# Cross-attention and a routed feed-forward block on one core: another order for the input transposes, the block product and its scaling

## The chip, the core and the metric

The kernel runs on one core of one Trainium2 chip. The metric is device time in microseconds (us), the median of several runs. Before the change it is 903.54 us (three runs, 903.44 to 903.98). Five queues of instructions run side by side, each in its own order: TensorE (PE in the profile, with its weight loads PEld), VectorE (DVE), ScalarE (ACT), GpSimd (POOL) and SyncE (SP), which here only issues DMAs. They meet at semaphores.

## What is computed

The input x has 128 batch elements of 128 rows by 256 features; ctx has the same shape. Per batch element:

```python
x = x + xattn(layernorm(x), ctx)   # 16 heads of 16: q from x, k and v from ctx
                                   # softmax over axis=2 of bhqk: over the QUERIES
x = x + ffn(layernorm(x))          # scores = x @ w_router; the 96 best rows of 128 become
                                   # gelu(row @ w_block), the other 32 rows stay as they are
```

## The kernel before, in words

**Slots.** Batch elements go through a software pipeline. One slot of the loop, `s`, runs the scores of element `s`, the attention of `s - 1`, the output projection and residual of `s - 2`, the transposes of the residual stream of `s - 3`, the block product (feed-forward weight) of `s - 4`, GELU of `s - 5` to `s - 7`, the routing of a group of eight elements, the final sum of `s - 16`, and, ahead of time, the normalising and transposing of the inputs of `s + 8`. Slots 0 and 1 and part of 2 and 3 are the start-up, written out by hand. Nothing plans the order at run time: each engine's function lists its calls by hand, the loops over `s` on PE (L567), ACT (L727), DVE (L1033), POOL (L1278) and SP (L310) each give one slot, and all else is semaphore waits. In the flag `sure` (slots 20 to 119 on PE) some waits are dropped that others imply.

**What the change and the prediction's steps touch.**

- `transpose_inputs` (L397, PE): four 128x128 transposes of the normalised input and of ctx into `ps_t`. `inputs_high` (L653, ACT) casts `ps_t` to the high part `t_hi`, `inputs_low` (L868, DVE) makes the rest, `t_lo`.
- `block_product` (L472, PE): six matmuls of 258 columns, also into `ps_t`. `product_scaled` (L931, DVE) scales it by the row's `rstd2` into `z_sb`. One PSUM bank thus serves the inputs and the product in turn.
- `queries_or_keys` (L504, PE): in each slot one half of the queries or keys of the next four elements, six matmuls of 512 columns into `ps_q`. `queries` or `keys` (L901, L913, DVE) empties the bank. `transpose_x1` (L417, PE) writes into the same bank and waits for that.
- `values` (L456), `projection` (L518), `scores` (L372), `attention` (L437): the other PE steps.
- `maxima` (L800, DVE): four reductions a slot, one for each quarter of the scores; `exps` (L635, ACT): four calls of four exponentials, the last quarter of element `s - 1` in slot `s`.
- `residual` (L821, DVE), then `stats2_of_pair` (L830, DVE): statistics for the second normalisation, once for two elements, in odd slots at the end. `stats1_of_pair` (L847): the same for inputs, in even slots.
- `rstd1_of_pair` (L1131), `rstd2_of_pair` (L1174, both POOL): powers from these statistics. `values_over_sums` (L1160, POOL) divides the values by the softmax sums into `v_pad`, which the attention matmuls need. `scaled_values_ready` (L433, PE) is the wait for it.
- `router` (L950, DVE): eleven steps spread over eight slots.

The order of PE in a slot before, and of POOL:

```python
scores(s); transpose_inputs(s + LEAD); values(s - 1); queries_or_keys(s); keep_columns; candidates
projection(s - 2); block_product(s - 4); scaled_values_ready(s - 1); transpose_x1(s - 3); attention(s - 1)

normalise(s + 9); rstd1_of_pair(s + 11); rstd2_of_pair(s - 4); gelu_square; values_over_sums(s - 1)
unprocessed; gelu_factor; gelu_sum; input_and_bias; gelu_cubic(s - 5); gelu_product(s - 7)
```

Of the kernel before, what the change touches and what calls it, by code (L numbers as in the profile page):

```python
# [6 lines left out]
def cross_attention_routed_ffn(  # L7
# [20 lines left out]
    B, T, E = x.shape  # L28
# [22 lines left out]
    with ctx:  # L51
# [93 lines left out]
        def has(b):  # L145
            return 0 <= b < B
# [86 lines left out]
        def _(sp):  # L233
# [64 lines left out]
            load_x(10)  # L298
            load_x(12)
            load_x(14)  # L300
            load_c(8)
            load_c(10)
            queries_even_odd_of_pair(2)
            load_c(12)
            load_c(14)
            queries_even_odd_of_pair(4)
            load_x(16)
            queries_even_odd_of_pair(6)
# [14 lines left out]
        def _(pe):  # L323
# [73 lines left out]
            def transpose_inputs(b, settled=False):  # L397
# [3 lines left out]
                if not settled:  # L401
                    inputs_ready(b)
                if has(b - LEAD - 5):
                    pe.wait_ge(z_ready, upto(b - LEAD - 5))
                elif 2 <= b <= 4:
                    pe.wait_ge(t_lo_ready, upto(b - 2))
                elif b > 4:
                    pe.wait_ge(t_lo_ready, upto(b - 1))
# [63 lines left out]
            def block_product(b, settled=False):  # L472
# [3 lines left out]
                if not settled:  # L476
                    pe.wait_ge(xt_ready, upto(b))
                pe.wait_ge(t_lo_ready, upto(b + LEAD + 4))
                if has(b - 1) and not has(b + LEAD + 4):
                    pe.wait_ge(z_ready, upto(b - 1))  # L480
# [86 lines left out]
            for s in range(2, B - 1):  # L567
                sure = 20 <= s < B - 8
                scores(s)
                if s < 4:  # L570
                    transpose_inputs(2 * s + 4)
                else:
                    transpose_inputs(s + LEAD, s > 4)
                values(s - 1)
                if s < 4:
                    queries_or_keys_of_pair(2 * s, 1)
                else:
                    queries_or_keys(s)
                keep_columns(s - 16)
                candidates(s - 12)  # L580
                projection(s - 2, sure)
                queries_and_keys_ready(s + 1)
                if s < 4:
                    transpose_inputs(2 * s + 5)
                if s == 2:
                    queries_or_keys_of_pair(6, 0)
                if s >= 4:
                    inputs_ready(s + LEAD + 1)
                block_product(s - 4, sure)
                if sure:  # L590
                    scaled_values_ready(s - 1)
                transpose_x1(s - 3, sure)
                router_bank_free(s + 1)
                attention(s - 1, sure)

            scores(B - 1)
            values(B - 2)
            projection(B - 3)
            block_product(B - 5)
            transpose_x1(B - 4)  # L600
# [17 lines left out]
        def _(act):  # L618
# [108 lines left out]
            for s in range(2, B):  # L727
                sure = 20 <= s < B - 1
                x1_high(s - 4, sure)
                exps(s - 1, 0, halves=(0,))  # L730
                attention_copy(s - 2, sure)
                exps(s - 1, 0, halves=(1,))
                gelu_tanh(s - 7)
                inputs_high(s + LEAD if s >= 4 else 2 * s + 4)
                exps(s, 3, sure)
                exps(s, 2)
                if s < 4:
                    inputs_high(2 * s + 5)
                exps(s, 1)
# [31 lines left out]
        def _(dve):  # L771
# [158 lines left out]

            def product_scaled(b, settled=False):  # L931

                if has(b):
                    dve.wait_ge(z_mm, upto(b))
                    if not settled:
                        dve.wait_ge(rstd2_ready, upto(b))
                    if b % 2 == 0 and has(b - R):
# [95 lines left out]
            for s in range(2, B):  # L1033
                sure = 20 <= s < B - 1
                x1_low(s - 4)
                if s == 3:
                    block_weights_low()
                router(s - 13, 2)
                router(s - 14, 4)
# [5 lines left out]
                values_and_bias(s - 1, sure)  # L1045
                inputs_low(s + LEAD if s >= 4 else 2 * s + 4)
                inverse_sums_01(s - 1)
# [10 lines left out]
                maxima(s, 0)  # L1058
                if s < 4:
                    inputs_low(2 * s + 5)  # L1060
                if s == 2:
# [10 lines left out]
                if s >= 4:  # L1072
                    stats1_of_pair(s + 12)
                product_scaled(s - 4, sure)
                if s < 4:
# [43 lines left out]
        def _(pool):  # L1119
# [8 lines left out]
            nc.gpsimd.memset(q_eo[:, 0, :, :, 2:4, :], 0.0).then_inc(q_eo_zero, 1)  # L1128
            nc.gpsimd.memset(q_eo[:, 1, :, :, :, :], 0.0).then_inc(q_eo_zero, 1)

# [128 lines left out]
            input_and_bias(0)  # L1259
            input_and_bias(1)  # L1260
            rstd1_of_pair(6)
            normalise(6)
# [7 lines left out]
            for s in range(2, 4):  # L1270
# [4 lines left out]
                input_and_bias(s + 2)  # L1275
            rstd1_of_pair(14)

            for s in range(4, B):  # L1278
                sure = 20 <= s < B - 1
                normalise(s + LEAD + 1, sure)  # L1280
                rstd1_of_pair(s + 11)
                rstd2_of_pair(s - 4)
                gelu_square(s - 5, sure)
# [4 lines left out]
                gelu_sum(s - 7)  # L1288
                input_and_bias(s + 2)
                gelu_cubic(s - 5)  # L1290
                gelu_product(s - 7)

            rstd2_of_pair(B - 4)
            gelu_factor(B - 5)
# [43 lines left out]
```

## Time and profile before

| | |
|---|---|
| median of three runs | 903.54 us |
| the profiled execution | 904.1 us, of which its span (first to last instruction) 902.3 us |
| busy share of the span | PE 96%, DVE 95%, ACT 96%, POOL 88% |
| granted TensorE clock, mean | 0.991 of full speed |
| DMA engines | 26.4% for the kernel's main queue |

How to read the rows below. A timeline row has the start in us, the length in us, the engine, the line, the operation, what is written and read, shapes, how many like instructions are merged (x16), and in brackets the idle time of the engine just before it and who ended it. Matmuls overlap in the pipeline, so the time that one costs is the distance from its start to the start of the next. On ACT, DVE and POOL a row's length also contains some overlap with the next row. A window row has the stretch, its length, then busy us (and instructions) of PE, PEld, DVE, ACT and POOL, the granted clock, and share and GB/s of the DMA engines. A wait row has the us in total, the times, and the longest.

### The profile page before, as it was taken

Reading aid. Unit: us, or ns where it says so; the run is one execution under the profiler, and the core shown is the slowest. Engines: PE = TensorE matmul, PEld = TensorE weight load, DVE = VectorE, ACT = ScalarE, POOL = GpSimd, SP = SyncE. Lnnn points to the kernel's source line nnn. Section 1 sums busy time; section 2 is a strip of 40 time slices with the busy share of each in tenths; the row PEclk is TensorE's granted clock in tenths of the full one; section 3 lists DMA queues with packets and bytes.
Section 4 is the critical chain, followed back from the end, with each engine's and each line's share of the span. In section 5 each row is a group of like instructions: output and inputs, shape, how many; then the busy total and the mean of one; then the engine's idle time right before and its main releaser. Section 6 shows DMA issues by size and latency. Waiting matters only on the chain. (4 is left out here: it accounts for less than half of the span.)

```text
span 902.3 us, 30174 instructions
## 1 busy us (share of the span) xinstructions
PE 864.8 (96%) x9842; PEld 718.8 (80%) x9842; DVE 857.9 (95%) x2068; ACT 870.6 (96%) x4632; POOL 789.6 (88%) x1489
## 2 busy tenths in 40 slices
PE   6999999999999999999999999999999999999972
PEld 6778888888888888888888888888888888888752
DVE  5888999999999999999999999999999999999987
ACT  4999999999999999999999999999999999999984
POOL 5468879999999999999999999999999999998865
PEclk9999999999999999999999999999999999999997
DMA  7221123232323232223333222323222323211102
GB/s 233 69 65 53 54 63 86 79 93 59 84 82 89 72 96 69 79 79 85 84 83 91 57 80 88 91 72 95 61 85 79 87 78 90 75 40 40 41 24 94
DMA packets 71357, 70.40 MB, mean 78 GB/s; under 512 B 12064, under 2 KB 63520, under 8 KB 71200
## 3 DMA queue, kind: packets, MB, share of 16 engines
q1 hardware_dynamic: 69840, 67.68, 26.4%
q8 instruction: 79, 1.29, 0.6%
q10 hardware_dynamic: 1360, 0.79, 0.3%
q14 instruction: 78, 0.64, 0.2%
HBM read 35.13 MB, written 16.78 MB: 58 GB/s over the span
## 5 line engine op out<-in xcount | busy, mean ns | idle before, releaser
L646 ACT ACTIVATE e_sb<-ps_s,neg_max 128x128 f32<-128x128 f32 x2048 | 772.1, 639 | 2.8 <-DVE neg_max L805 2.7
L646 ACT ACTIVATION_READ_ACCUMULATOR e_sb<-ps_s,neg_max 128x1 f32 x2048 | 718.2, 464 | 0.0
L805 DVE TENSOR_REDUCE neg_max<-ps_s 128x4 f32<-128x512 f32 x512 | 331.0, 666 | 19.7 <-PE ps_s L385 18.2
L385 PE MATMUL ps_s<-q_eo,k_sb 32*128 32x256 f32 x2048 | 146.6, 399 | 3.6 <-ACT e_sb L646 1.5
L450 PE MATMUL ps_a<-e_sb,v_pad 128*32 128x128 f32 x4096 | 138.4, 276 | 1.5 <-POOL v_pad L1168 0.9
L344 PE MATMUL ps_a<-w_o_sb,o_sb 128*128 128x256 f32 x512 | 131.7, 379 | 4.0 <-DVE v_sb L929 3.8
L450 PEld LDWEIGHTS ps_a<-e_sb,v_pad 128*32 128x32 f32 x4096 | 104.1, 109 | 23.2 <-issue 21.5
L385 PEld LDWEIGHTS ps_s<-q_eo,k_sb 32*128 32x128 f32 x2048 | 95.8, 184 | 32.9 <-issue 28.7
L344 PEld LDWEIGHTS ps_a<-w_o_sb,o_sb 128*128 128x128 f32 x512 | 93.8, 189 | 22.8 <-issue 4.7
L1157 POOL TENSOR_TENSOR x_sb<-x_sb,bo_sb 128x256 f32<-128x256 f32 x128 | 105.1, 822 | 0.2
L1168 POOL TENSOR_TENSOR v_pad<-v_sb,recip 128x256 f32<-128x256 f32 x128 | 79.5, 621 | 29.1 <-DVE recip L865 27.1
L657 ACT CAST t_hi<-ps_t 128x512 fp32r<-128x512 f32 x126 | 94.3, 748 | 7.5 <-PE ps_t L414 7.0
L688 ACT ACTIVATE g_sb<-g_sb 128x256 f32<-128x256 f32 x128 | 99.0, 774 | 1.4 <-POOL g_sb L1215 1.4
L337 PE MATMUL ps_t<-w_z_hi,xt_hi 128*128 128x258 f32 x256 | 96.4, 377 | 2.2 <-DVE z_sb L941 2.2
L665 ACT COPY o_sb<-ps_a 128x256 f32<-128x256 f32 x128 | 91.1, 712 | 2.4 <-PE ps_a L450 2.4
L633 ACT CAST xt_hi<-ps_q 128x256 fp32r<-128x256 f32 x128 | 88.4, 691 | 1.4 <-PE ps_q L430 1.4
L1215 POOL TENSOR_TENSOR g_sb<-g_sb,z_sb 128x256 f32<-128x256 f32 x128 | 88.3, 690 | 0.3
L873 DVE TENSOR_TENSOR t_lo<-ps_t,t_hi 128x512 fp32r<-128x512 f32 x126 | 85.2, 676 | 2.7 <-ACT t_hi L657 2.6
L337 PE MATMUL ps_a<-w_v_hi,t_hi 128*128 128x256 f32 x256 | 83.2, 325 | 0.7 <-DVE w_z_sb L797 0.7
L1229 POOL TENSOR_TENSOR z_sb<-g_sb,z_sb 128x256 f32<-128x256 f32 x121 | 82.8, 684 | 0.0
L1198 POOL TENSOR_TENSOR g_sb<-z_sb 128x256 f32<-128x256 f32 x123 | 75.3, 612 | 0.0
L337 PE MATMUL ps_a<-w_v_lo,t_hi 128*128 128x256 f32 x256 | 72.5, 283 | 0.0
(113 smaller groups left out, 2213.8 us busy)
## 6 DMA issues: line engine op xcount, KB each, us to landing
x_sb<-in_x SPq DMA_DIRECT2D x64, 256.0 KB, 3.0
c_sb<-in_ctx SPq DMA_DIRECT2D x64, 256.0 KB, 3.0
out<-z_sb SPq DMA_DIRECT2D x64, 256.0 KB, 2.4
q_eo<-q_raw SPq DMA_DIRECT2D x504, 32.0 KB, 2.0
z_sb<-in_L_xattn_Wkv ACTq DMA_DIRECT2D x2, 256.0 KB, 6.7
z_sb<-in_L_xattn_Wq ACTq DMA_DIRECT2D x1, 256.0 KB, 3.6
w_z_sb<-in_L_ffn_w_block SPq DMA_DIRECT2D x1, 256.0 KB, 8.0
w_o_sb<-in_L_xattn_Wo SPq DMA_DIRECT2D x1, 256.0 KB, 7.1
```

Source lines behind the costliest of these rows:

```text
L337: last = nc.tensor.matmul(dst, lhs(a, c), rhs(b, c), start=(c == 0 and n == 0), stop=(c == C - 1 and n == len(terms) - 1))
L344: last = nc.tensor.matmul(dst, lhs(c), rhs(c), start=(c == 0), stop=(c == C - 1))
L385: mm = nc.tensor.matmul(ps_s[:, bank(b, j), c, :, :], k_sb[rows, r2, c, h * T:(h + 1) * T], q_eo[rows, r2, :, c, h, :], start=True, stop=True)
L450: mm = nc.tensor.matmul(ps_attn[32 * j:32 * j + 32, c * T:(c + 1) * T], v_pad[:, b % 2, c * J + j, par:par + 2, :].rearrange("p a d -> p ( ...
L633: nc.scalar.copy(xt_hi[:, b % 2, :], ps_xt).then_inc(xt_hi_ready, 1)
L646: last = nc.scalar.activation(e_sb[:, b % 3, j, c, par, :], ps_s[:, bank(b, j), c, par, :], ACT.Exp, bias=neg_max[:, b % 4, h:h + 1], accu ...
L657: nc.scalar.copy(t_hi[:, n, :, :, h * T:(h + 1) * T].rearrange("p k c t -> p (k c) t"), inputs_bank(b)[:, :].rearrange("p (n t) -> p n t", ...
L665: nc.scalar.copy(o_sb[:, b % 2, :], ps_attn).then_inc(o_ready, 1)
L688: nc.scalar.activation(g_sb[:, b % 4, :], g_sb[:, b % 4, :], ACT.Tanh, scale=SLOPE).then_inc(tanh_ready, 1)
L805: nc.vector.tensor_reduce(neg_max[:, b % 4, :].rearrange("p (c j q) -> p j c q", c=C, j=J)[:, j, :, :], ps_s[:, bank(b, j), :, :, :], AX.X ...
L1157: nc.gpsimd.tensor_tensor(x_sb[:, b % RX, :], x_sb[:, b % RX, :], bo_sb[:, :], ALU.add).then_inc(xb_ready, 1)
L1215: nc.gpsimd.tensor_tensor(g_sb[:, b % 4, :], g_sb[:, b % 4, :], z_sb[:, b % R, 0:E], ALU.mult).then_inc(cubic_ready, 1)
```

## The change

On PE, the transposes of the inputs go from behind the scores to the end of the slot, between the transposes of the residual stream and the attention. The block product goes from behind the projection to a place between the values and the queries or keys. On DVE its scaling goes from the end of the slot to a place between the second and the third maximum, and the low part of the inputs goes to the top of the slot. On ACT the cast of the inputs goes to the top of the slot, and the last quarter of the exponentials is no longer split by the copy of the attention. On POOL `rstd2_of_pair` goes from before `values_over_sums` of the next slot to a place ahead of `gelu_cubic`, and `rstd1_of_pair` from odd to even slots. The bounds of two waits move by one. In the start-up SP issues some loads behind the queries' DMAs instead of ahead of them, one memset of POOL comes later, and the second inputs of slots 2 and 3 are cast a slot later.

```diff
 sync (start-up)
             load_x(12)
+            queries_even_odd_of_pair(2)
+            load_c(8)
             load_x(14)
-            load_c(8)
             load_c(10)
-            queries_even_odd_of_pair(2)
+            queries_even_odd_of_pair(4)
             load_c(12)
+            load_x(16)
             load_c(14)
-            queries_even_odd_of_pair(4)
-            load_x(16)
             queries_even_odd_of_pair(6)
 tensor: transpose_inputs(b)
-                if has(b - LEAD - 5):
-                    pe.wait_ge(z_ready, upto(b - LEAD - 5))
+                if has(b - LEAD - 4):
+                    pe.wait_ge(z_ready, upto(b - LEAD - 4))
 tensor: block_product(b)
-                pe.wait_ge(t_lo_ready, upto(b + LEAD + 4))
+                pe.wait_ge(t_lo_ready, upto(b + LEAD + 3))
 tensor: loop over s
                 scores(s)
                 if s < 4:
                     transpose_inputs(2 * s + 4)
-                else:
-                    transpose_inputs(s + LEAD, s > 4)
                 values(s - 1)
+                block_product(s - 4, sure)
...
                 projection(s - 2, sure)
                 queries_and_keys_ready(s + 1)
-                if s < 4:
-                    transpose_inputs(2 * s + 5)
-                if s == 2:
-                    queries_or_keys_of_pair(6, 0)
                 if s >= 4:
-                    inputs_ready(s + LEAD + 1)
-                block_product(s - 4, sure)
+                    inputs_ready(s + LEAD)
                 if sure:
                     scaled_values_ready(s - 1)
                 transpose_x1(s - 3, sure)
+                transpose_inputs(s + LEAD if s >= 4 else 2 * s + 5, s >= 4)
                 router_bank_free(s + 1)
                 attention(s - 1, sure)
+                if s == 2:
+                    queries_or_keys_of_pair(6, 0)
             scores(B - 1)
             values(B - 2)
+            block_product(B - 5)
             projection(B - 3)
-            block_product(B - 5)
 scalar: loop over s
                 x1_high(s - 4, sure)
-                exps(s - 1, 0, halves=(0,))
+                if s == 3:
+                    inputs_high(9)
+                elif s >= 4:
+                    inputs_high(s + LEAD - 1)
                 attention_copy(s - 2, sure)
-                exps(s - 1, 0, halves=(1,))
+                exps(s - 1, 0)
                 gelu_tanh(s - 7)
-                inputs_high(s + LEAD if s >= 4 else 2 * s + 4)
+                if s < 4:
+                    inputs_high(2 * s + 4)
                 exps(s, 3, sure)
                 exps(s, 2)
-                if s < 4:
-                    inputs_high(2 * s + 5)
                 exps(s, 1)
 vector: loop over s
                 x1_low(s - 4)
                 if s == 3:
                     block_weights_low()
+                    inputs_low(9)
+                elif s >= 4:
+                    inputs_low(s + LEAD - 1)
...
                 maxima(s, 3)
                 maxima(s, 2)
                 router(s - 16, 9)
                 values_and_bias(s - 1, sure)
-                inputs_low(s + LEAD if s >= 4 else 2 * s + 4)
+                if s < 4:
+                    inputs_low(2 * s + 4)
+                product_scaled(s - 4)
                 inverse_sums_01(s - 1)
                 maxima(s, 1)
...
                 maxima(s, 0)
-                if s < 4:
-                    inputs_low(2 * s + 5)
...
                 stats2_of_pair(s - 3)
                 if s >= 4:
                     stats1_of_pair(s + 12)
-                product_scaled(s - 4, sure)
 gpsimd (start-up)
-            nc.gpsimd.memset(q_eo[:, 1, :, :, :, :], 0.0).then_inc(q_eo_zero, 1)
...
             input_and_bias(1)
+            nc.gpsimd.memset(q_eo[:, 1, :, :, :, :], 0.0).then_inc(q_eo_zero, 1)
             rstd1_of_pair(6)
...
-            rstd1_of_pair(14)
+            rstd2_of_pair(0)
 gpsimd: loop over s
                 normalise(s + LEAD + 1, sure)
-                rstd1_of_pair(s + 11)
-                rstd2_of_pair(s - 4)
+                rstd1_of_pair(s + 10)
                 gelu_square(s - 5, sure)
                 values_over_sums(s - 1, sure)
...
                 input_and_bias(s + 2)
+                rstd2_of_pair(s - 3)
                 gelu_cubic(s - 5)
                 gelu_product(s - 7)
 gpsimd (end)
-            rstd2_of_pair(B - 4)
```

`product_scaled` also waits for `rstd2_ready` in every slot now, where it left that wait out in the `sure` ones.

## Rows read from the trace of the kernel before

**Rows 1.** Busy time by engine in a stretch of eight slots.

```profile
448.74:502.22 53.48, 53.20 (x621) 44.27 (x615) 52.67 (x130) 53.48 (x293) 49.97 (x96) 1.00 0.29 81
```

**Rows 2.** Timeline of PE in slot 66, up to the scores of slot 67.

```profile
462.89 1.15 PE L385 MATMUL ps_s<-q_eo,k_sb 32*128 32x256 f32 x16
...
465.19 0.39 PE L337 MATMUL ps_q<-t_hi,w_k_hi 128*128 128x512 f32 x1
...
466.34 0.39 PE L337 MATMUL ps_q<-t_lo,w_k_hi 128*128 128x512 f32 x1
466.56 1.02 PE L344 MATMUL ps_a<-w_o_sb,o_sb 128*128 128x256 f32 x4
...
467.55 0.28 PE L337 MATMUL ps_t<-w_z_hi,xt_lo 128*128 128x258 f32 x1
...
468.15 0.38 PE L430 MATMUL ps_q<-ident,x_sb 128*128 128x128 f32 x2
468.46 1.08 PE L450 MATMUL ps_a<-e_sb,v_pad 128*32 128x128 f32 x32
469.47 1.15 PE L385 MATMUL ps_s<-q_eo,k_sb 32*128 32x256 f32 x16
```

**Rows 3.** Timeline of DVE in slot 67, an odd slot.

```profile
470.76 1.29 DVE L805 TENSOR_REDUCE neg_max<-ps_s 128x4 f32<-128x512 f32 x2 [0.23 <-PE ps_s L385]
...
473.57 0.74 DVE L918 TENSOR_SCALAR k_sb<-ps_q,bk_sb 128x512 f32<-128x512 f32 x1
474.23 0.41 DVE L827 TENSOR_TENSOR x_sb<-ps_a,x_sb 128x256 f32<-128x256 f32 x1
...
475.62 0.70 DVE L834 BATCH_NORM_STATS2 st<-x_sb 128x6 f32<-128x512 f32 x1
```

**Rows 4.** Timeline of POOL in slots 67 and 68.

```profile
470.12 0.64 POOL L1215 TENSOR_TENSOR g_sb<-g_sb,z_sb 128x256 f32<-128x256 f32 x1
...
471.97 0.19 POOL L1136 TENSOR_SCALAR ve<-st 128x2 f32<-128x2 f32 x1
...
473.68 0.62 POOL L1168 TENSOR_TENSOR v_pad<-v_sb,recip 128x256 f32<-128x256 f32 x1
...
476.62 0.72 POOL L1215 TENSOR_TENSOR g_sb<-g_sb,z_sb 128x256 f32<-128x256 f32 x1
...
478.65 0.19 POOL L1179 TENSOR_SCALAR ve<-st 128x2 f32<-128x2 f32 x1
...
479.65 0.61 POOL L1198 TENSOR_TENSOR g_sb<-z_sb 128x256 f32<-128x256 f32 x1
```

**Rows 5.** Timelines where one engine was released by another: DVE, PE; DVE, POOL.

```profile
403.42 0.46 DVE L941 TENSOR_SCALAR z_sb<-ps_t,rstd 128x258 f32<-128x258 f32 x1
...
403.94 0.44 PE L414 MATMUL ps_t<-ident,xhat 128*128 128x128 f32 x2 [0.19 <-DVE z_sb L941]
...
874.78 0.69 DVE L834 BATCH_NORM_STATS2 st<-x_sb 128x6 f32<-128x512 f32 x1
...
875.63 0.19 POOL L1179 TENSOR_SCALAR ve<-st 128x2 f32<-128x2 f32 x1 [1.07 <-DVE st L834]
```

**Rows 6.** Groups of instructions by line: a router step (mean ns of one).

```profile
L967 DVE MAX8 top<-cand 8x8 f32<-8x128 f32 x64 | 17.5, 273 | 0.4
```

**Rows 7.** Start-up: timelines of ACT, PE and POOL, and a wait of SP.

```profile
38.05 0.59 ACT L657 CAST t_hi<-ps_t 128x512 fp32r<-128x512 f32 x1 [0.69 <-PE ps_t L414]
...
46.17 0.59 ACT L657 CAST t_hi<-ps_t 128x512 fp32r<-128x512 f32 x1 [0.87 <-PE ps_t L414]
...
48.31 1.15 PE L385 MATMUL ps_s<-q_eo,k_sb 32*128 32x256 f32 x16 [0.94 <-ACT e_sb L646]
...
25.01 0.19 POOL L1136 TENSOR_SCALAR ve<-st 128x2 f32<-128x2 f32 x1 [9.04 <-DVE st L851]
...
SPq L263 <- DVE q_raw L886: 4.5, 1, 4.5
```

**Rows 8.** Busy time by engine in two early stretches; the granted clock follows the five engines.

```profile
11.00:15.20 4.20, 3.88 (x20) 3.88 (x21) 2.43 (x5) 1.11 (x3) 3.60 (x8) 0.59 1.11 356
...
20.50:27.30 6.80, 4.32 (x37) 3.44 (x36) 5.88 (x13) 6.06 (x36) 2.10 (x5) 1.00 0.16 35
```

More of the change, by code:

```diff
@@ L477, in block_product @@
                     pe.wait_ge(xt_ready, upto(b))
-                pe.wait_ge(t_lo_ready, upto(b + LEAD + 4))
-                if has(b - 1) and not has(b + LEAD + 4):
+                pe.wait_ge(t_lo_ready, upto(b + LEAD + 3))
+                if has(b - 1) and not has(b + LEAD + 3):
                     pe.wait_ge(z_ready, upto(b - 1))
@@ L929, in values_and_bias, with product_scaled @@
                     nc.vector.tensor_tensor(v_sb[:, b % 2, :], ps_v, bv_sb[:, :], ALU.add).then_inc(v_ready, 1)
-            def product_scaled(b, settled=False):
+            def product_scaled(b):
                 if has(b):
                     dve.wait_ge(z_mm, upto(b))
-                    if not settled:
-                        dve.wait_ge(rstd2_ready, upto(b))
+                    dve.wait_ge(rstd2_ready, upto(b))
                     if b % 2 == 0 and has(b - R):
```

## The prediction, made before the changed kernel was run

> **What bounds the kernel now.** First I read the busy time of eight slots in the middle [rows 1]. ACT is busy for 53.48 of 53.48 us: it never pauses, and 53.48/8 gives 6.69 us a slot, 13.37 us for two. The reader should see that nothing in the steady state can shorten a slot without taking work from ACT; the change only reorders ACT's work. The other engines are close behind: PE misses 0.3 us of the stretch, DVE 0.8, POOL 3.5. So I asked next how long a new order lets a loop of waits between these engines become, and read one slot of each in the timelines [rows 2 to 4]. Beyond 13.37 us for two slots, such a loop takes over from ACT.
>
> PE's slot [rows 2]. From the scores to the first matmul of the keys are 2.30 us. That is the scores (1.15), four input transposes and six values. Five matmuls of the block product take 0.60 us (467.55 to 468.15), so one of 256 columns 0.12 and six values 0.72; the four transposes are left with 0.43. The rest: keys 1.37, projection 0.87, product 0.72, residual transposes and the turn to the attention 0.31, attention 1.01. The sum is 6.58, just what the slot took, 0.1 below ACT.
>
> **The change part by part.** Time zero is PE's start of the scores in an odd slot.
>
> *The product ahead of the keys.* Scores and values without the transposes take 2.30 - 0.43 = 1.87, the product 0.72, the keys 1.37: the last key matmul has streamed at 3.96. Its record ends 0.17 later than the next step starts (466.34 + 0.39 against 466.56 [rows 2]), at 4.13. DVE wakes 0.14 after PE's last record (469.47 + 1.15 against 470.76 [rows 2, 3]) and empties the bank in 0.74 [rows 3]: 4.27 to 5.01. PE wakes 0.06 after DVE (403.88 to 403.94 [rows 5]). Only then may it transpose the residual stream, whose bank this is. Before, projection and product (1.59 us) covered that; now only the projection (0.87) does, up to 4.83. PE stands 0.24 us (without that, its slot would be 6.57), and behind it in its queue stand both groups of transposes and the attention: 5.07 + 0.31 + 0.43 + 1.01 = 6.82 us for a slot. DVE is at the keys in time: before the change it started them 4.10 us after the scores (473.57 - 469.47).
>
> *The statistics moved ahead of GELU on POOL.* This is the large term. `stats2_of_pair` is still the end of DVE's odd slot, and the residual ahead of it needs this slot's projection: record end 3.96 + 1.02 = 4.98, DVE at 5.12, from the residual to the statistics 1.39, the statistics 0.70 [rows 3]: 7.21. POOL wakes 0.16 later (875.47 to 875.63 [rows 5]). Before, it did cubic, product and the next normalising first, and came to the statistics 2.03 us later (476.62 to 478.65 [rows 4]), when they had long been there. Now `rstd2_of_pair` stands ahead of these three, so POOL waits, and all that is queued behind starts from 7.37: rstd2 1.00 (478.65 to 479.65), the three 2.03, then, since `rstd1_of_pair` is now in even slots too, rstd1 with the square 1.71 (471.97 to 473.68), and only then the scaled values, 0.62 [rows 4]. They are ready at 12.73. Before, in slot 68, they were ready at 479.65 + 0.57 + 0.62, which is 4.7 us after its scores at 476.14; now at 12.73 - 6.82 = 5.91. (0.57 is POOL's square, 473.11 to 473.68 as part of the 1.71; I take it the same.)
>
> *Who waits for that.* PE's next slot, in the `sure` slots already ahead of the residual transposes. Woken at 12.79, it does 0.31 + 0.43 + 1.01 and is at the next odd slot's scores at **14.54 us**. Every edge of this loop is the order of one queue or a datum, so it closes: with these durations two slots cannot be shorter. Against 13.37 that is 1.17 us more for two slots; ACT, now with time to spare, waits for the maxima.
>
> *The sum.* Slots 20 to 119 are 50 pairs: 58.5. In two odd slots of eight a router step (0.27 [rows 6]) stands on DVE between keys and statistics: 0.54 for each of 12.5 groups, 6.8. In slots 4 to 19 and 120 to 123 PE waits for the scaled values only at the attention, so the loop is 12.79 + 1.01 = 13.80: 0.43 for each of 10 pairs, 4.3.
>
> *Start-up.* ACT waits 0.69 and 0.87 us for transposes in slots 2 and 3, and PE's scores of slot 4 then wait 0.94 for ACT [rows 7]. Casting a slot later takes both waits from ACT's way. In slot 2 PE itself sets the pace, so I count only the last: -0.9, bounds 0 and -1.6. SP's loads go behind eight DMAs for the queries, which waited 4.5 us for DVE [rows 7]; the first load is used by transposes that stand behind the scores of slot 2, which wait for these DMAs themselves, so nothing; were that cover gone, a wait of up to those 4.5. The memset lands in a stretch where POOL waits 9.04 us [rows 7]: nothing, and nothing saved where it stood, as the statistics set that start.
>
> *Nothing else.* The low part of the inputs takes on DVE the place ahead of the maxima that the scaling had; 0.3 us more there lies in the wait for PE's scores (0.23 [rows 3]) and the slack of a longer slot. The unsplit exponentials are the same instructions. At the end, POOL's wait of 1.07 us [rows 5] may go, or a later product may cost as much: 0, bounds -1.1 and +1.1.
>
> 58.5 + 6.8 + 4.3 - 0.9 = 68.7 us. The profiled execution was 904.1 us, 0.6 above the median; on the median this is **972 us**.
>
> *Bounds.* Values right behind scores, and a weight load after a wait, have no row; nearest are the turns in rows 2, so -0.1 or +0.2 for two slots. POOL's three links took only 1.85 in slot 67 (470.12 to 471.97 [rows 4]): -0.18. The two hand-overs that I put at 0.06 may take 0.16: +0.2. The router may fit into slack: -6.8. So the pair is 14.26 to 14.94, and the sum 46 to 93: 950 to 997.
>
> **The rivals.**
>
> (B) *Scaled values in time.* If POOL reaches the statistics without a wait, or its chain is shorter by a microsecond, the loop of PE and DVE alone is left: 6.82 a slot, 13.64 for two, 0.27 for each of 60 pairs, less 0.9: 919. For it: POOL misses 3.5 us of eight slots [rows 1]. Against: its wait is for DVE, not for its own work.
>
> (C) *Faster.* ACT stays the bound, because PE's stand in a slot is covered by the queue ahead of ACT, and the start-up gives both casts' waits back (1.56) and the end POOL's wait (1.07): 903.5 - 2.6 = 901. It decides at one point: whether PE leaves the attention within 13.37 us for two slots. For it: 6.82 is only 0.13 above ACT's slot, within the errors. Against: the two-slot loop is 1.17 above, nine times that.
>
> (D) *No change.* Transposes and scaling are only shifted within slots, ACT keeps its pace, and start-up and end give nothing: 903.5. The same point speaks against it.
>
> (E) *The clock falls.* In an early stretch the granted clock was 0.59, mostly at the lower level of 1.2 GHz, after PE had waited for POOL; in a later one with pauses (PE busy 4.32 of 6.80) it stayed at 1.00, the level of 2.4 GHz [rows 8]. With PE's 5.7 us of the loop at half speed, two slots would take 20 us and the kernel some 1300. PE would stand 14.54 - 2 x 6.57 = 1.4 us in two slots, a smaller share than in the later stretch, so I hold it unlikely. The Trainium skill (TensorE: Matmul & The Clock Gate, "A second HAM failure mode: psum-queue depth-cycling") says that short pauses between groups of matmuls that wait for PSUM can make the clock swing between its levels; by that rule E comes. The later stretch here has such pauses and disagrees.
>
> **How the numbers follow.** Chances: the forecast 0.80, B 0.08, C 0.06, D 0.04, E 0.02. The loop rests on measured pitches of four queues and on no guess about timing, hence the 0.80; its own range, 950 to 997, I hold to be right nine times in ten, which is 0.72. With B (917 at the least) it is 0.80: the range is 917 to 997. A measurement of this kernel tells 0.2% from no change: 901.7 and below is faster, 905.3 and above slower. Faster is C, 0.06; same is D, 0.04; slower is the forecast, B and E, 0.90.
>
> **What would show it.** ACT's share falls to 13.37/14.54, some 92%, with waits for DVE's maxima. The distance of scores alternates: about 6.8 from an odd to an even slot, 7.7 from an even one on. PE waits in even slots for `v_pad`, in odd ones for DVE's keys or queries. POOL waits in every odd slot for the statistics. If scores come every 6.7 us with ACT full, the loop is wrong; if all slots are 6.8, only its POOL part is.

## The result, and the profile after

The changed kernel takes 985.13 us (median of 4 runs, 983.69 to 985.36), the kernel before 903.76 us on the same chip (4 runs, 903.44 to 904.68): a ratio of 1.089, 95% interval 1.088 to 1.091. Slower, as forecast, by 81.4 us where 68.7 was forecast; the range held the time. The profiled execution took 983.69 us, its span is 981.9.

A first look at the page of after: busy time and share of each engine. Line numbers of after lie up to 3 below those of before.

```profile
PE 885.5 (90%) x9842; PEld 702.4 (72%) x9842; DVE 890.9 (91%) x2068; ACT 896.0 (91%) x4632; POOL 778.6 (79%) x1489
```

No engine is full any more: ACT has fallen from 96% to 91%, and the same work is done. Eight slots in the middle (60 to 67 here, where [rows 1] has 64 to 71), busy time by engine, the granted clock behind the five engines:

```profile
454.91:514.53 59.62, 54.66 (x611) 43.29 (x612) 55.33 (x129) 55.41 (x291) 49.15 (x94) 1.00 0.26 72
```

Eight slots take 59.62 us instead of 53.48, every engine pauses for 4 us or more, and the clock is at its full level (1.00). This is what a loop of waits looks like on a page: all engines lose share together. The view of waits of after names the edges (us in total, times, longest):

```profile
POOL ve L1178 <- DVE st L833: 69.1, 62, 1.9
POOL v_pad L1167 <- DVE recip L864: 67.6, 65, 6.1
PE ps_q L430 <- POOL v_pad L1167: 54.8, 49, 1.3
ACT o_sb L662 <- PE ps_a L450: 29.3, 72, 1.9
ACT xt_hi L630 <- PE ps_q L430: 21.2, 51, 0.7
```

POOL waits for the statistics 62 times, once in nearly every pair of slots, and PE waits 49 times for the scaled values, once in each pair of the `sure` slots but the last. The wait in the second row lies in odd slots, ahead of POOL's wait for the statistics, and so costs nothing here. ACT waits behind them for PE's results. The timelines of one pair show the loop. First PE, from an even slot's scores to the next even slot's (start, length, instruction, idle time before and its releaser):

```profile
501.38 1.15 PE L385 MATMUL ps_s<-q_eo,k_sb 32*128 32x256 f32 x16
...
507.51 0.41 PE L430 MATMUL ps_q<-ident,x_sb 128*128 128x128 f32 x2 [1.12 <-POOL v_pad L1167]
507.75 0.38 PE L414 MATMUL ps_t<-ident,xhat 128*128 128x128 f32 x2
...
508.28 1.08 PE L450 MATMUL ps_a<-e_sb,v_pad 128*32 128x128 f32 x32
509.29 1.15 PE L385 MATMUL ps_s<-q_eo,k_sb 32*128 32x256 f32 x16
...
513.04 0.39 PE L337 MATMUL ps_q<-t_lo,w_k_hi 128*128 128x512 f32 x1
513.27 1.02 PE L344 MATMUL ps_a<-w_o_sb,o_sb 128*128 128x256 f32 x4
514.43 0.41 PE L430 MATMUL ps_q<-ident,x_sb 128*128 128x128 f32 x2
...
516.21 0.50 PE L385 MATMUL ps_s<-q_eo,k_sb 32*128 32x256 f32 x4
```

The even slot takes 7.91 us (501.38 to 509.29), the odd one 6.92 (509.29 to 516.21). In the even slot PE stands 1.12 us ahead of the residual transposes for `v_pad`; in the odd slot it stands ahead of the same transposes for the bank of the keys. That one is DVE's to empty, in the same odd slot:

```profile
513.53 0.75 DVE L917 TENSOR_SCALAR k_sb<-ps_q,bk_sb 128x512 f32<-128x512 f32 x1 [0.26 <-issue]
514.33 0.42 DVE L826 TENSOR_TENSOR x_sb<-ps_a,x_sb 128x256 f32<-128x256 f32 x1
...
515.84 0.69 DVE L833 BATCH_NORM_STATS2 st<-x_sb 128x6 f32<-128x512 f32 x1
```

DVE waits 0.26 us and ends at 514.28; PE starts at 514.43. The trace names no releaser for either; the last key matmul's record ends 0.10 us before DVE starts. The statistics end at 516.53. POOL from there on, into the next even slot:

```profile
516.69 0.19 POOL L1178 TENSOR_SCALAR ve<-st 128x2 f32<-128x2 f32 x1 [1.06 <-DVE st L833]
...
517.70 0.74 POOL L1214 TENSOR_TENSOR g_sb<-g_sb,z_sb 128x256 f32<-128x256 f32 x1
...
519.75 0.19 POOL L1135 TENSOR_SCALAR ve<-st 128x2 f32<-128x2 f32 x1
...
521.46 0.62 POOL L1167 TENSOR_TENSOR v_pad<-v_sb,recip 128x256 f32<-128x256 f32 x1
```

POOL waits 1.06 us, does its chain without a pause and has the scaled values at 522.08; PE starts its transposes 0.26 us later:

```profile
522.34 0.41 PE L430 MATMUL ps_q<-ident,x_sb 128*128 128x128 f32 x2 [1.01 <-POOL v_pad L1167]
```

**Where the 79.6 us of span came from** (981.9 against 902.3), from the starts of the scores in both traces. Slots 20 to 115: 59.62 for eight slots against 53.50, twelve times: +73.4. Slots 4 to 19: +4.8. Slots 116 to 123: +3.3. From slot 124: -0.2. From the scores of slot 0 to those of slot 4: 31.77 against 31.03, +0.75. And the first scores come 2.55 us earlier; that last part is not the change's (see the kernel before run again, below).

### The profile page after: what moved, and what is told of

It reads as the page before. It is cut to its first block and busy times, and to the rows that moved or that the text cites. A ratio compares the mean times of both kernels' runs of the same rounds, so it can differ in the third digit from the quotient of the medians.

```text
span 981.9 us, 30179 instructions
## 1 busy us (share of the span) xinstructions
PE 885.5 (90%) x9842; PEld 702.4 (72%) x9842; DVE 890.9 (91%) x2068; ACT 896.0 (91%) x4632; POOL 778.6 (79%) x1489
## 5 line engine op out<-in xcount | busy, mean ns | idle before, releaser
L643 ACT ACTIVATE e_sb<-ps_s,neg_max 128x128 f32<-128x128 f32 x2048 | 693.7, 450 | 2.9 <-DVE neg_max L804 2.7
L643 ACT ACTIVATION_READ_ACCUMULATOR e_sb<-ps_s,neg_max 128x1 f32 x2048 | 548.3, 275 | 0.0
L430 PE MATMUL ps_q<-ident,x_sb 128*128 128x128 f32 x256 | 52.3, 286 | 64.1 <-POOL v_pad L1167 54.8
L430 PEld LDWEIGHTS ps_q<-ident,x_sb 128*128 128x128 f32 x256 | 26.0, 140 | 109.9 <-issue 109.4
L654 ACT CAST t_hi<-ps_t 128x512 fp32r<-128x512 f32 x126 | 88.6, 703 | 8.9 <-PE ps_t L414 5.7
L1156 POOL TENSOR_TENSOR x_sb<-x_sb,bo_sb 128x256 f32<-128x256 f32 x128 | 93.8, 734 | 0.5 <-DMA bo_sb<-in_L_xattn_bo 0.3
L992 DVE SCALAR_TENSOR_TENSOR z_sb<-z_sb,half_keep,x_sb 128x256 f32<-128x256 f32 x128 | 74.1, 584 | 16.3 <-POOL x_sb L1246 16.0
L662 ACT COPY o_sb<-ps_a 128x256 f32<-128x256 f32 x128 | 48.7, 380 | 35.9 <-PE ps_a L450 29.3
L630 ACT CAST xt_hi<-ps_q 128x256 fp32r<-128x256 f32 x128 | 61.8, 483 | 21.2 <-PE ps_q L430 21.2
L337 PEld LDWEIGHTS ps_a<-w_v_hi,t_hi 128*128 128x128 f32 x256 | 47.9, 187 | 42.6 <-issue 42.0
```

Of the source, the lines that this page charges most:

```text
L337: last = nc.tensor.matmul(dst, lhs(a, c), rhs(b, c), start=(c == 0 and n == 0), stop=(c == C - 1 and n == len(terms) - 1))
L643: last = nc.scalar.activation(e_sb[:, b % 3, j, c, par, :], ps_s[:, bank(b, j), c, par, :], ACT.Exp, bias=neg_max[:, b % 4, h:h + 1], accu ...
L654: nc.scalar.copy(t_hi[:, n, :, :, h * T:(h + 1) * T].rearrange("p k c t -> p (k c) t"), inputs_bank(b)[:, :].rearrange("p (n t) -> p n t", ...
L1156: nc.gpsimd.tensor_tensor(x_sb[:, b % RX, :], x_sb[:, b % RX, :], bo_sb[:, :], ALU.add).then_inc(xb_ready, 1)
```

## The experiments

Each ran beside the kernel before, on one chip with it: 904.24 us (7 runs) beside the first four, 902.43 (7) beside the next four, 902.0 (7) beside the two after them, 903.41 (15) beside the last.

**One edge of the POOL loop opened.** The chain between statistics and scaled values is cut by 1.14 us in even slots: `rstd1_of_pair` goes back to odd slots.

```
             rstd2_of_pair(0)
+            rstd1_of_pair(14)
...
-                rstd1_of_pair(s + 10)
+                rstd1_of_pair(s + 11)
```

> The changed kernel with one thing put back: the input statistics' power (rstd1_of_pair) runs in odd slots again, so that it no longer stands between rstd2 and the scaled values of the even slots. My theory (two-slot loop through POOL): the loop loses POOL's 1.14 us, v_pad of the even slot is ready some 11.65 us after the odd scores, the even slot falls below the loop of PE and DVE, and all slots last about 6.92 us (measured odd slot of the changed kernel) instead of 6.93 and 7.97: 985 - 50 x 1.0 = 930 to 937 us. Rival R1 (rstd2's wait for the statistics alone costs the time, rstd1's place does not matter): about 985. Rival R2 (the transposes at the end of PE's slot are what lengthens it, by themselves): about 985.

Measured: 940.22 us, ratio 1.039 (1.038 to 1.041). PE's waits for the scaled values fell from 54.8 to 3.4 us:

```profile
PE ps_q L430 <- POOL v_pad L1167: 3.4, 12, 0.3
```

Eight slots take 56.0 us, the plain slots 6.92 to 6.94: what is left is the loop over the bank of the keys. The time is 3 us above the expectation: slots with router steps take 7.1 to 7.25. There DVE never pauses and comes to the queries late; PE stands for them:

```profile
472.50 0.41 PE L430 MATMUL ps_q<-ident,x_sb 128*128 128x128 f32 x2 [0.51 <-DVE q_raw L909]
```

In the profiled execution the way from the scores of slot 0 to those of slot 4 is also 1.46 us longer than in the changed kernel (33.23 against 31.77). That belongs to this execution: the granted clock fell there, where the changed kernel has 1.00 in the same stretch, and with the same edit in the experiment with both loops opened it is 31.96.

```profile
41.00:46.00 5.00, 5.00 (x26) 4.71 (x26) 3.31 (x7) 3.94 (x22) 1.36 (x3) 0.66 0.20 43
```

So 45 of the 81 us hang on these 1.14 us of POOL.

**PE's input transposes ahead of its waits.**

```
+                transpose_inputs(s + LEAD if s >= 4 else 2 * s + 5, s >= 4)
                 if sure:
                     scaled_values_ready(s - 1)
                 transpose_x1(s - 3, sure)
-                transpose_inputs(s + LEAD if s >= 4 else 2 * s + 5, s >= 4)
```

> The changed kernel with the input transposes ahead of the wait for the scaled values and of the residual transposes, instead of behind both. My theory: they fill PE's wait for DVE's keys (odd slots fall from 6.93 to about 6.6 to 6.7) and no longer stand in the POOL loop: two slots 14.89 - 0.44 = about 14.45, so 50 x 0.44 less: about 963 us (958 to 970). Rival R1: the same. Rival R2 (transposes at the end of the slot are the cause as such): 985, no change. Rival R3 (PE's wait for the keys is the main loss, both slots): about 904 to 915.

Measured: 962.72 us, ratio 1.065 (1.063 to 1.066), as expected. The 0.43 us of transposes now lie in both waits: odd slots 6.60 to 6.75, even ones 7.67 to 7.96. That the pair falls by 0.39 in the mean, near the 0.44 expected, is partly luck. One pair of four takes 14.26 instead of 14.83, since besides the transposes the hand-over from POOL's scaled values to PE has become shorter, 0.05 us instead of 0.26. The other three take 14.51 to 14.71: DVE does not pause in their odd slots and ends the statistics 7.5 to 7.7 us after the odd scores, not 7.24.

**The wait for the scaled values only at the attention.** `scaled_values_ready(s - 1)` is taken out of the loop, and `attention(s - 1)` waits for itself in all slots.

> The changed kernel with the early wait for the scaled values ahead of the residual transposes taken out; the attention waits for them itself in every slot, as slots 4 to 19 do already. My theory: both groups of transposes run while POOL works, the even slot ends 1.0 us earlier, two slots last about 13.85 as in slots 4 to 19 of the changed kernel (6.93 each): 985 - 50 x 1.0 = 930 to 938 us. Rivals R1 and R2: about 985, because the attention has to wait for the same datum. Rival R3 (the wait for the keys): about 985.

Measured: 955.20 us, ratio 1.057 (1.055 to 1.058). Missed: eight slots take 57.2 us instead of about 55.5. The two largest waits behind POOL's in its view of waits:

```profile
DVE z_sb L990 <- POOL x_sb L1244: 20.9, 43, 0.9
ACT e_sb L641 <- DVE neg_max L802: 20.9, 52, 1.4
```

(Line numbers lie 2 below those of the changed kernel.) The 30 us that this gives show that the place of the wait matters. What is left is another two-slot loop, of DVE and POOL without PE. DVE's `final` (L990) waits for a POOL instruction that stands behind the scaled values (L1244); from there DVE runs to the end of the statistics, and POOL back to that instruction, neither with a pause above 0.15 us:

```profile
494.99 0.72 DVE L990 SCALAR_TENSOR_TENSOR z_sb<-z_sb,half_keep,x_sb 128x256 f32<-128x256 f32 x1 [0.59 <-POOL x_sb L1244]
...
502.42 0.69 DVE L831 BATCH_NORM_STATS2 st<-x_sb 128x6 f32<-128x512 f32 x1
...
503.27 0.19 POOL L1176 TENSOR_SCALAR ve<-st 128x2 f32<-128x2 f32 x1 [1.05 <-DVE st L831]
...
508.66 0.56 POOL L1244 TENSOR_SCALAR x_sb<-x_sb,alpha,beta 128x256 f32<-128x256 f32 x1
...
509.26 0.72 DVE L990 SCALAR_TENSOR_TENSOR z_sb<-z_sb,half_keep,x_sb 128x256 f32<-128x256 f32 x1 [0.32 <-POOL x_sb L1244]
```

One turn takes 14.27 us (494.99 to 509.26); the four turns of eight slots take 14.10 to 14.57, together the 57.2. The expectation knew only the loop through PE. In the changed kernel this one is hidden behind the 14.83.

**POOL's order alone, in the kernel before.** Only the POOL lines of the diff, with everything else as before.

> The kernel before, with the changed order of POOL alone (rstd2 ahead of the cubic at the end of odd slots, rstd1 in even slots, nothing else changed). My theory: statistics end 6.85 us after the odd scores, POOL 0.16 + 1.00 + 2.05 + 1.71 + 0.62 to the scaled values at 12.39, hand-over 0.26, residual transposes 0.33, attention 1.01: two slots 14.0 against 13.37, 50 x 0.63 = 31 and a few for the router: 930 to 942 us. Rival R2 (PE's new order as such): 904, no change. Rival R1 (rstd2's wait): the same as mine.

Measured: 937.53 us, ratio 1.037 (1.035 to 1.038), as expected. Eight slots take 56.3 us, a pair 14.1 in the mean and a plain one 13.85. PE waits for the scaled values here too, though its own order is the old one:

```profile
PE ps_q L430 <- POOL v_pad L1168: 27.1, 49, 0.8
```

So the two-slot loop does not need PE's new order. The rest of the change makes it 0.98 us longer (14.83 against 13.85 for a plain pair). The edges that differ, POOL to PE and DVE's statistics (the odd scores start at 485.10, the next odd ones at 498.94):

```profile
483.05 0.62 POOL L1168 TENSOR_TENSOR v_pad<-v_sb,recip 128x256 f32<-128x256 f32 x1
483.72 0.44 PE L430 MATMUL ps_q<-ident,x_sb 128*128 128x128 f32 x2 [0.47 <-POOL v_pad L1168]
...
491.25 0.70 DVE L834 BATCH_NORM_STATS2 st<-x_sb 128x6 f32<-128x512 f32 x1
```

The statistics end 6.85 us after the odd scores instead of 7.24; PE starts its transposes 0.05 us behind the scaled values instead of 0.26; and from there to the next odd scores it takes 1.38 us instead of 1.78, as the input transposes do not stand there. The expectation had put the hand-over at 0.26.

**Everything but POOL's order.** The reverse: the changed kernel with POOL's lines as before.

> The changed kernel with POOL's order of before (rstd1 a pair further ahead in odd slots, rstd2 behind normalise and rstd1, the same at start and end); PE, ACT, DVE and SP as changed. Theory: without POOL's part only the loop of PE and DVE over the keys' bank is left, 6.92 to 6.97 us a slot, eight slots 55.4 to 56.0, the kernel 927 to 936 us; the product's scaling on DVE waits for rstd2 in even slots (some 0.5 us) without carrying it further. Rival 1, this wait of DVE delays sums, scaled values and PE: eight slots above 57, over 950 us. Rival 2, PE's wait for the keys is covered by the queue ahead of ACT: eight slots 53.5, about 902 to 905 us.

Measured: 947.99 us, ratio 1.050 (1.048 to 1.052): between my two values, so the theory was short of something. Five slots of eight take 6.93 to 7.00, the loop over the keys' bank. Slots 0 to 2 of eight take 7.1 to 7.5. Slots 0 and 1 have router steps, and DVE does not pause in them. In slot 2 of eight it waits; DVE's timeline in slot 66, with POOL's `rstd2` and PE:

```profile
485.93 0.70 POOL L1180 TENSOR_TENSOR rstd<-ve,minus_half 128x2 f32<-128x2 f32 x1
486.72 0.49 DVE L939 TENSOR_SCALAR z_sb<-ps_t,rstd 128x258 f32<-128x258 f32 x1 [0.64 <-issue]
487.12 0.19 DVE L864 RECIPROCAL recip<-sums 128x8 f32<-128x8 f32 x1
487.23 0.64 DVE L804 TENSOR_REDUCE neg_max<-ps_s 128x4 f32<-128x512 f32 x1
487.79 0.74 DVE L917 TENSOR_SCALAR k_sb<-ps_q,bk_sb 128x512 f32<-128x512 f32 x1
488.68 0.41 PE L430 MATMUL ps_q<-ident,x_sb 128*128 128x128 f32 x2 [0.51 <-DVE k_sb L917]
```

The scaling, now in the middle of DVE's slot, waits 0.64 us for `rstd2`, which ends 0.09 us before it starts; DVE reaches the keys 4.62 us after the scores (483.17) instead of 4.24 in the changed kernel, and PE stands for it. I had called that wait harmless. DVE waits so 14 times in the run, 8.9 us in all. POOL's early `rstd2` thus spares the new place of the scaling a wait in one slot of eight, and it is also what closes the other loop. The two halves cost 33.3 and 45.6 us alone; their sum lies near the 81.4 of the whole, but the losses are not the same ones.

**Both loops opened.** The first two experiments together.

> Both edits together in the changed kernel: the statistics behind the inputs' normalising run a pair further ahead in odd slots (as in the experiment with rstd1 alone), and PE transposes the inputs ahead of its waits (as in the experiment with the inputs first). Theory: the change made two loops, PE-DVE over the keys' bank (6.92 us a slot) and the two-slot loop over POOL (14.83); the input transposes (0.43) cover the wait for the keys, and POOL's chain without rstd1 lets PE's attention end at about 13.1 us of two slots. Both loops then lie under ACT's 13.37, so eight slots take 53.4 to 54.0 us and the kernel 901 to 908 us. Rival 1, the key loop stays in another form (DVE late with the keys because its own slot is full): eight slots 55 to 56, 920 to 935 us. Rival 2, the scaled values are still late: eight slots above 56, over 935 us.

Measured: 911.79 us, ratio 1.010 (1.009 to 1.012). 73 of the 81 us are gone, so nine tenths of the change's loss hang on these two loops. The time is 4 us above my theory and 8 below the first rival. Six slots of eight take 6.60 to 6.75, around ACT's pace of 6.69; two take 7.12 and 6.91. In the slot that begins at 451.11 DVE runs from end to end without a pause and comes to the queries at 455.76, 4.65 us after the scores:

```profile
454.70 0.47 DVE L939 TENSOR_SCALAR z_sb<-ps_t,rstd 128x258 f32<-128x258 f32 x1
455.10 0.18 DVE L864 RECIPROCAL recip<-sums 128x8 f32<-128x8 f32 x1
455.20 0.63 DVE L804 TENSOR_REDUCE neg_max<-ps_s 128x4 f32<-128x512 f32 x1
455.76 0.73 DVE L909 TENSOR_SCALAR q_raw<-ps_q,bq_sb 128x512 f32<-128x512 f32 x1
...
456.64 0.41 PE L430 MATMUL ps_q<-ident,x_sb 128*128 128x128 f32 x2
457.11 1.08 PE L450 MATMUL ps_a<-e_sb,v_pad 128*32 128x128 f32 x32
```

PE starts its transposes 0.15 us behind the queries, and its attention 0.15 us behind the residual that DVE does next (it ends at 456.96). So the rival that DVE is late with the keys holds in two slots of eight. The scaling's place does not explain it: in the kernel before, the low part stood there, 0.60 us long, and between the statistics and the queries DVE does the same instructions in the same slot, also without a pause, 4.51 us from start to start against 4.69 here. It came to the queries 4.22 us after the scores because its statistics began 0.29 us ahead of them, not 0.04. Why DVE is further behind PE here no run isolates.

**The start: loads and memset as before.** SP's order of loads and the place of POOL's memset undone in the changed kernel.

> The changed kernel with the order of SP's loads and the place of POOL's memset at the start as before. Theory: both were priced at nothing, so the time is that of the changed kernel, 983 to 987 us (ratio to the kernel before 1.088 to 1.092), and scores of slot 4 lie 31.5 to 32.1 us behind the scores of slot 0, as in the changed kernel (31.8). Rival: the loads' new order is what makes the start of the changed kernel shorter by 2 us or longer by 0.8: then the distance falls to 31.0 or the time rises to 987 to 989 us.

Measured: 983.67 us, ratio 1.090 (1.088 to 1.092), as expected; scores of slot 4 come 31.78 us behind those of slot 0, in the changed kernel 31.77. Both edits cost nothing, as priced.

**The kernel before, once more.**

> The kernel before, once more with a profile. Theory: the first scores at 17.3 us and the low granted clock between 11 and 15 us are a matter of the execution and not of the code: in this execution the scores of slot 0 may come at 14.7 to 15.4 us as in the changed kernel and all experiments, and the scores of slot 4 then lie 30.9 to 31.2 us behind them (31.0 before). Rival: they belong to the kernel before, and the scores of slot 0 come at 17.2 to 17.4 us again.

Measured: 902.47 us (one run). The first scores come at 15.47 us, a little later than expected, but not at 17.29 as in the first execution, and from there to the scores of slot 4 it is 31.03 us in both. The stretch that had a granted clock of 0.59 in [rows 8] now reads 1.00:

```profile
11.00:15.20 4.20, 3.94 (x32) 3.70 (x32) 3.36 (x7) 2.63 (x6) 2.62 (x6) 1.00 1.11 362
```

So the early low clock, and with it 1.8 of the 2.55 us by which the changed kernel's first scores were earlier, belongs to the execution and not to the code. The rest lies within what the executions with a granted clock of 1.00 in this stretch show: first scores between 14.54 and 15.47 us.

**The queries of slot 2 at their old place.** In the changed kernel PE does them behind the attention of slot 2. The timelines there, of DVE and PE:

```profile
38.20 0.69 DVE L885 TENSOR_TENSOR q_raw<-ps_q,bq_sb 128x512 f32<-128x512 f32 x1 [2.49 <-issue]
38.81 0.20 DVE L857 RECIPROCAL recip<-ps_s 128x8 f32<-128x8 f32 x1
...
39.06 1.15 PE L385 MATMUL ps_s<-q_eo,k_sb 32*128 32x256 f32 x16 [0.95 <-DVE recip L857]
```

```
                 queries_and_keys_ready(s + 1)
+                if s == 2:
+                    queries_or_keys_of_pair(6, 0)
                 if s >= 4:
                     inputs_ready(s + LEAD)
...
                 attention(s - 1, sure)
-                if s == 2:
-                    queries_or_keys_of_pair(6, 0)
```

> The changed kernel with one step undone: in slot 2 PE does the queries of the pair from block 6 ahead of its waits and of the attention again, as before. Theory: behind the attention they come so late that DVE waits 2.49 us for them, and behind that wait in DVE's queue stand the inverse sums that free the bank for the scores of slot 3; so slot 2 grew from 7.95 to 9.15 us. Then slot 2 falls to 7.9 to 8.2 us, scores of slot 4 come 30.4 to 30.9 us behind those of slot 0 (31.8 in the changed kernel, 31.0 before), and the time falls by 0.8 to 1.3 us against the changed kernel (983.7 to 985.1) and no more. Rival: another step (the casts of the inputs a slot later, or the transposes at the end of the slot) sets slot 2, which stays at 9.1 us.

Measured: 982.46 us (4 runs, 980.90 to 983.60), ratio 1.089 (1.087 to 1.091). The time alone can't tell 1 us, the less so as the granted clock of the profiled execution fell to 0.57 at 954 to 958 us, and its slots from 124 on took 54.09 us against 52.99 in the changed kernel. The start of the trace does tell it: slot 2 falls from 9.15 to 7.95 us, slot 3 from 7.45 to 7.04, and scores of slot 4 come 30.15 us behind those of slot 0:

```profile
37.10 0.69 DVE L885 TENSOR_TENSOR q_raw<-ps_q,bq_sb 128x512 f32<-128x512 f32 x1 [0.88 <-issue]
```

DVE's wait of 2.49 is 0.88. That is 1.63 us for the moved queries, more than the 0.9 to 1.4 expected, and 0.88 us less than the kernel before.

**Both loops opened, and the queries at their old place.**

> The experiment with both loops opened (911.8 us), and the queries of the pair from block 6 at their earlier place as well. Theory: slots 4 to 127 as there (eight slots 54.1), the start shorter by 0.8 to 1.3 us: 910.3 to 911.3 us, ratio to the kernel before 1.008 to 1.010. What remains over the kernel before (903) are two slots of eight in which DVE never pauses (7.12 and 6.91 us) and the last slots. Rival: with the start in step the later slots fall into the pace of ACT as well, 904 to 907 us.

Measured: 910.81 us, ratio 1.010 (1.008 to 1.011), as expected. The start is shorter by 1.6 us, eight slots stay at 54.1.

**The later casts alone, in the kernel before.** The one part of the change that gained anything in the trace, tried without the rest: ACT and DVE cast the second inputs of slots 2 and 3 at the head of the next slot.

```
                 x1_high(s - 4, sure)
+                if s in (3, 4):
+                    inputs_high(2 * s + 3)
                 exps(s - 1, 0, halves=(0,))
...
-                if s < 4:
-                    inputs_high(2 * s + 5)
                 exps(s, 1)
```

(and the same for `inputs_low` on DVE)

> The kernel before with one part of the change alone: in the start-up the second inputs of slots 2 and 3 are cast at the head of the next slot (ACT's high part and DVE's low part), everything else as before. Theory: this part is worth what its two waits on ACT cost (0.69 and 0.87 us, of which the last reaches PE), and it came out as a loss in the changed kernel only because of the moved queries. Then scores of slot 4 come 30.1 to 30.5 us behind those of slot 0 (31.0 before), later slots keep 53.5 us for eight, and the kernel is 0.5 to 0.9 us shorter, ratio 0.9985 to 1.000, within what a measurement can tell from no change. Rival: PE needs these inputs earlier in the old order of its transposes, the start stays at 31.0 us or becomes longer.

Measured: 903.76 us (11 runs), ratio 1.0005 (0.9996 to 1.0014): no difference that can be told. The start is 30.79 us instead of 31.03, less gained than the 0.5 to 0.9 expected: PE's wait of 0.94 for ACT [rows 7] is gone, but PE now waits for the cast in slot 3:

```profile
39.93 0.41 PE L414 MATMUL ps_t<-ident,xhat 128*128 128x128 f32 x2 [0.71 <-DVE t_lo L873]
```

In the profiled execution slots 4 to 115 took 1.7 us more than in both executions of the kernel before (750.5 against 748.8); why stays open.

No version beat the kernel before.

## Why the prediction was right, and where it was off

**The loop over POOL** is shown: its edges stand in the trace in the order in which they were added up, and taking 1.14 us out of it gave 45 us. Counted from the odd scores at 509.29: statistics done 7.24 (forecast 7.21), POOL starts 7.40 (7.37), scaled values ready 12.79 (12.73), PE turns 0.26 later (0.06), next odd scores 14.83 (14.54). The term that was mis-sized is "PE wakes 0.06 after DVE" used for POOL as well: it measured 0.26, above the 0.16 that the bounds allowed it, and is 0.20 of the 0.29 that a pair lacked. It is not that POOL hands over more slowly: the same pair of engines took 0.05 with PE's order of before, and 0.05 with the input transposes ahead of the wait. 49 pairs at 0.29 are 14.2 us, more than the 12.7 that the forecast lacked. Against it, the router steps cost 0.30 us for eight slots, not 0.54 (eight slots measured 59.62, four plain pairs make 59.32), which is 3 us less in all, and in the last `sure` pair PE did not wait for the scaled values. By the prediction's own terms the upper end of its sum is 95, not 93 (78.5 + 6.8 + 4.3 + 4.5 + 1.1); the measured 81.4 lies below both. Rivals C and D, which let two slots stay within 13.37 us, are out.

**The loop over the bank of the keys** is shown too: keys done at 4.14 after the scores (forecast 4.13, record end 513.43), DVE at 4.24 (4.27), PE 0.15 behind DVE's end (0.06), a slot of 6.92 (6.82). With the POOL loop opened and nothing else, 6.92 to 6.94 is the plain slot. Rival B had this loop alone at 919; with POOL's chain cut the kernel took 940, since the hand-over is longer (0.1 us a slot, 12 us), DVE has no time left in router slots (some 8 us), and the start-up did not gain.

**Slots 4 to 19** came out at 6.93 us each as the mean of slots 4 to 11, 13.86 for a pair against 13.80 forecast, but by the other loop. In the timelines there PE waits for the keys in odd and even slots alike, and not for the scaled values. The number was right, the step was not: the statistics of an odd slot start 6.1 us after its scores there, not 6.55 as later, since DVE's `final`, which stands ahead of them, begins only with slot 16; so POOL's chain starts earlier. In slots 9 and 10, whose scores start at 81.17 and 88.11, the scaled values are ready at 93.50, and PE stands for the keys until 93.25 and reaches its attention only at 94.03:

```profile
87.27 0.66 DVE L833 BATCH_NORM_STATS2 st<-x_sb 128x6 f32<-128x512 f32 x1
92.88 0.62 POOL L1167 TENSOR_TENSOR v_pad<-v_sb,recip 128x256 f32<-128x256 f32 x1
```

**The start-up** was wrong in its sum, +0.75 instead of -0.9, and the step that failed is one that was left out. "In slot 2 PE itself sets the pace" held before the change. The text priced the casts, loads and memset, and gave no price to the queries that are moved behind the attention. They cost 1.63 us: a late bank for DVE, and behind DVE's wait the sums that free the next scores. With the queries back, the start gained 0.88 us, as forecast: PE's wait of 0.94 for ACT is gone. In the kernel before the casts alone take this wait away too, but 0.71 us of it comes back as PE's wait for the cast, and 0.24 are left; which other part of the change keeps that wait at 0.29 no run isolates. Loads and memset: nothing, as priced.

**Of the signs to look for**, the alternation of slots (6.93 and 7.97 in the mean, 6.8 and 7.7 forecast), PE's waits in even slots and POOL's in odd ones are there. ACT's share, 91%, is near the 92% forecast. One was wrong: ACT waits for PE's results (29.3 and 21.2 us) and only 2.7 us for DVE's maxima, in four waits.

**The clock.** With a pause of some 1.1 us in every pair the granted clock of the steady stretch is 1.00, 2.4 GHz, and 0.993 over the run, so rival E is out. The rule of the Trainium skill (TensorE: Matmul & The Clock Gate, "A second HAM failure mode: psum-queue depth-cycling") by which it would have come is not borne out by the steady stretches of this kernel, before or after. The granted clock did fall in the last 11 to 17 us of every execution, and once ahead of that in three: the kernel before (0.59 at 11 to 15.2 us) and two experiments (0.66 at 41 to 46, 0.57 at 954 to 958). It never swung to and fro.

## What to carry to other kernels

Before reordering a kernel in which the engines are nearly full, write the loop that the new queue orders close, over as many iterations as its conditions span (two here), and add up its edges from measured pitches; a chain of three engines that is 1.2 us too long is paid in every iteration and shows as idle time on all engines at once. Behind the longest loop there can be another one, a little shorter, that sets the pace once the first is opened (14.26 us behind 14.83 here). An instruction that is moved past another takes with it everything behind it in the queue of whoever waits for it, so each moved instruction gets a line in the sum, the one in the start-up too. Where a part's number comes out right, look at which wait set it.

## What the runs showed of the hardware

The hand-over from POOL's scaled values into PE's transposes took 0.26 us in the 49 waits of the changed kernel, 0.10 in the 12 waits left with `rstd1` back in odd slots, and 0.05 in the 49 waits each with the input transposes ahead and with POOL's order alone. From DVE's keys or queries it took 0.15 where PE waited in the new order, where [rows 5] show 0.06 from DVE. So one pair of engines has no single hand-over time; what sets it no run isolates. The records of busy time are not a measure of work alone: eight slots of the same work have 53.48 us of ACT in [rows 1] and 55.41 after the change. And the granted clock of 11 to 15 us differs between executions of the same program, 0.59 and 1.00, which moves all that follows by 1.8 us.
